# Graph attention on one core: each pair scored and mixed one step behind its decoding, with two gather buffers and two closing pairs

## The chip, the cores and the metric

The kernel runs on one core of a Trainium2 chip. The metric is the time of one execution on the device in microseconds (us), the median of several executions. A difference of about 0.2% (1.6 us) is what a measurement of this kernel can tell from none.

## What is computed

A layer of graph attention over 8192 nodes with 128 features, and a 0/1 matrix of 8192 x 8192 integers that says who is whose neighbour:

```python
h = jnp.maximum(_layernorm(x, axis=-1), 0.0)
s_i = h @ attn[:d]
s_j = h @ attn[d:]
e = leaky_relu(s_i + s_j.T, negative_slope=0.2)
e = e + jnp.where(adj > 0, 0.0, -1e9)
out = x + softmax(e, axis=1) @ h
```

The matrix is 256 MB. Each row has on average four neighbours, so the softmax of a row runs over a handful of nodes once they are known.

## The kernel before

**Start.** The nodes are read (4 MB), normalised in four quarters, and multiplied with the attention vectors. The result, `h` with its scores, is written to a table in DRAM, `h_table`, from which neighbours are later gathered.

**Stream.** The adjacency is read in 64 tiles of 128 rows, each in two halves of 2 MB. The halves are numbered n = 0 to 127 here; tile t has halves 2t and 2t+1, and two tiles make a pair p (halves 4p to 4p+3), so there are 32 pairs. A ring of five half buffers (`adj_ring`) takes the loads, which are issued on SP's queue (`load_pair`). The load of half n+5 is issued when ScalarE (ACT) has turned half n into signs (`sign_tile`, which also counts the row's neighbours).

**Decoding.** TensorE packs the signs of a tile into code words (`pack_tile`; three tiles in PSUM), VectorE (DVE) takes the largest words (`max_tile`), and after the pair's second tile derives from them the numbers of up to twelve neighbours for the pair's two rows in each partition (`find_pair`, whose last result is `near_id`). GpSimd (POOL) then issues twelve indirect DMAs that fetch these rows of `h_table` into a buffer of the ring `near` (`gather_pair`).

**Scoring and mixing.** `score_pair` (DVE) adds scores over the gathered rows and ends with `below`; `exp_pair` (ACT) makes the weights; `weigh_mix` and two `add_row` (DVE) sum the weighted rows and add x, which counts up `pair_mixed`. SP stores the pair. Pair g is scored in DVE's step g+2 (the table `MIXES`), between the two `max_tile` of that step, and mixed in the same step, around `flag_pair`. ACT computes its weights in the step after that, behind the first of four halves. The ring `near` has three buffers; gather p waits until pair p-3 is mixed.

**The rest.** Rows with too many neighbours for twelve slots go to a list of 128 rows for each eight pairs (the deep list: `find_deep`, `gather_m`, `score_deep`, `exp_m`, `add_deep`, `store_m`). Rows without a neighbour form the lone batch, in the last pairs (`lone_mark` to `lone_end`); its partial sums are added by `lone_add`, and TensorE's `rank_pair` of some pairs waits for that, because both use the same PSUM bank. The last three pairs (`CLOSING`) are not mixed by DVE: DVE's `weigh_pair` gives weights, ACT writes 16 diagonal matrices a pair (`write_diagonals`), TensorE multiplies (`mix_pair`), ACT copies out (`close_pair`). After the stream come the last deep list, a loop for rows that fit nowhere (one short round here) and the rest of the lone batch.

**Order.** Every engine's program is written out by hand in its own block, in order; semaphores are the only links. In one step p, DVE runs `lone_begin`, `max_tile(2p)`, scoring, `max_tile(2p+1)`, `key_pair`, `find_pair(p)`, the first row's sum, `flag_pair(p)`, `find_deep`, the lone batch, the second row's sum. The rows of the profile carry line numbers of the code below: L614 is the sign, L631 `exp_pair`, L770 `max_tile`, L822 `near_id`, L907 the first instruction of `score_pair`, L923 `below`, L1017 the first of `score_deep`, L1158 `lone_add`, L1367 `pack_tile`, L1385 `rank_pair`, L521 `gather_pair`.

## Time and profile before

| | us |
|---|---|
| median of three executions | 815.76 (815.68 to 815.86) |
| the profiled execution | 813.88 |
| its span, first to last instruction | 812.1 |
| ScalarE busy | 534.3 |
| VectorE busy | 615.4 |
| TensorE busy | 368.9 |
| GpSimd busy | 504.5 |

The profile is one execution. Its page gives busy times, the span in 40 slices of 20.3 us, the chain of work that ended last, and the costliest groups. The timeline lists instructions in order of time; each row has a start, a duration, the engine, the line, what is written and read, and in brackets how long the engine idled ahead of it and what released it.

### The profile page before, as it was taken

The numbers are of one execution on the slowest core, as the hardware profiler recorded it, in microseconds if no ns is written. First come the engines' busy times: TensorE is split into PE (matmuls) and PEld (weight loads), VectorE is DVE, ScalarE is ACT, GpSimd is POOL, SyncE is SP. The second block draws the span as 40 slices with busy tenths as digits, with TensorE's granted clock in tenths as the row PEclk, the third lists the DMA queues.
The fourth block names the chain that finished last, engine by engine and source line by source line (L and its number), as shares of the span: only waits on it lengthen the run. The fifth ranks groups of instructions, "written<-read, shape, count | busy, mean of one in ns | idle before, by whom it ended". The sixth has DMA issues, their size and how long they took to land.

```text
span 812.1 us, 6394 instructions
## 1 busy us (share of the span) xinstructions
PE 368.9 (45%) x1359; PEld 168.9 (21%) x1378; DVE 615.4 (76%) x2028; ACT 534.3 (66%) x410; POOL 504.5 (62%) x526
## 2 busy tenths in 40 slices
PE   1455334444433344444444344443444545646647
PEld 1222011111111111111111011111111213424636
DVE  6898288677758667797769666797769799898933
ACT  4985676676676767676675767667666677767430
POOL 6720777755556767755547677556547667765573
PEclk9875565555555555555555565555555556877679
DMA  8999999999999999999999999999999999993120
GB/s 344 406 408 429 393 406 408 405 414 411 410 391 412 411 408 406 405 406 407 410 403 406 409 407 408 407 412 413 411 412 408 409 407 411 406 410 132 33 56 8
DMA packets 39719, 301.59 MB, mean 371 GB/s; under 512 B 10682, under 2 KB 17149, under 8 KB 22272
## 3 DMA queue, kind: packets, MB, share of 16 engines
q1 hardware_dynamic: 24032, 277.04, 83.9%
q0 software_dynamic: 15360, 23.88, 8.6%
q10 hardware_dynamic: 288, 0.26, 0.1%
q8 instruction: 11, 0.18, 0.1%
q14 instruction: 28, 0.23, 0.1%
HBM read 303.76 MB, written 8.98 MB: 385 GB/s over the span
## 4 chain that ended last, share of the span: by engine, by line
DMA 74%; issue 14%; POOL 5%; ACT 3%; DVE 3%; PE 1%; POOLq 0%; SPq 0%; DVEq 0%
DMA adj_ring<-in_adj_dram 73%; POOL near L521 3%; ACT sign_ring L614 2%; POOL near_m L532 2%; DMA x_all<-in_x_dram 1%; DVE one_hot L725 1%; ACT h_all L626 1%; PE words L1367 0%; DMA out_dram<-adj_ring 0%; POOL out_dram L562 0%; DVE sums L955 0%; DVE cand L770 0%; POOLq L597 0%; DVE terms L950 0%; POOL adj_ring L553 0%
## 5 line engine op out<-in xcount | busy, mean ns | idle before, releaser
L614 ACT ACTIVATE sign_ring<-adj_ring,half_neg 128x4096 fp8e3<-128x4096 int32 x128 | 474.9, 3710 | 215.3 <-DMA adj_ring<-in_adj_dram 215.3
L521 POOL DMA_INDIRECT near<-h_table,near_id x384 | 391.1, 1019 | 234.2 <-issue 122.8
L1367 PE MATMUL words<-sign_ring,pack_w 128*128 128x512 bf16 x511 | 220.2, 581 | 357.9 <-ACT sign_ring L614 357.6
L770 DVE MAX8 cand<-words 128x8 f32<-128x256 f32 x256 | 90.8, 416 | 113.3 <-PE words L1367 113.3
L1367 PEld LDWEIGHTS words<-sign_ring,pack_w 128*128 128x128 bf16 x512 | 53.9, 125 | 520.7 <-ACT sign_ring L614 453.1
L955 DVE TENSOR_REDUCE sums<-terms 128x128 f32<-128x1024 f32 x58 | 112.2, 1935 | 2.0
L532 POOL DMA_INDIRECT near_m<-h_table,id_m x64 | 65.1, 1017 | 19.5 <-issue 19.5
L950 DVE TENSOR_TENSOR terms<-near,weight 128x512 f32<-128x512 f32 (+1 forms) x87 | 73.4, 871 | 0.0
L1358 PE MATMUL words<-place,place_w 128*128 128x512 bf16 x110 | 55.2, 587 | 7.1 <-DVE key L862 3.7
L1393 PEld LDWEIGHTS listing<-cand,one_hot 128*128 128x128 f32 x128 | 33.0, 316 | 10.6 <-issue 7.3
L1348 PE MATMUL listing<-h_all 128*1 128x128 f32 x128 | 18.6, 316 | 24.8 <-ACT h_all L626 24.8
L1393 PE MATMUL listing<-cand,one_hot 128*128 128x34 f32 x128 | 27.6, 358 | 0.2 <-DVE one_hot L866 0.2
L614 ACT ACTIVATION_READ_ACCUMULATOR sign_ring<-adj_ring,half_neg 128x1 f32 x128 | 23.8, 186 | 0.0
L1443 PE MATMUL rank<-h_all,x_all 128*64 128x129 f32 x128 | 21.0, 343 | 4.6 <-DVE key L862 4.6
L787 DVE TENSOR_TENSOR terms<-cand_i,code_mask 128x512 int32<-128x512 int32 x32 | 22.1, 692 | 1.1
L958 DVE SCALAR_TENSOR_TENSOR x_all<-sums,inv,x_all 128x128 f32<-128x128 f32 x58 | 20.4, 351 | 2.1
L756 DVE TENSOR_TENSOR near<-h_all,terms 128x2048 f32<-128x2048 f32 x8 | 21.4, 2681 | 0.0
L644 ACT ACTIVATE adj_ring<-ident,adj_ring 128x128 f32<-128x128 f32 x48 | 14.3, 387 | 10.7 <-DVE adj_ring L970 10.7
L1443 PEld LDWEIGHTS rank<-h_all,x_all 128*64 128x64 f32 x128 | 20.3, 181 | 4.9 <-DVE key L862 4.9
L626 ACT ACTIVATE h_all<-x_all,terms 128x128 f32<-128x128 f32 x48 | 18.8, 480 | 2.3 <-DVE terms L742 2.3
L498 POOL TENSOR_SCALAR h_all<-x_all,terms 128x128 f32<-128x128 f32 x16 | 13.0, 828 | 11.7 <-DVE terms L742 11.7
L907 DVE TENSOR_SCALAR score<-near,h_all 128x8 f32<-128x8 f32 x32 | 7.0, 220 | 17.1 <-DMA near<-h_table,near_id 17.1
(271 smaller groups left out, 521.7 us busy)
## 6 DMA issues: line engine op xcount, KB each, us to landing
adj_ring<-in_adj_dram SPq DMA_DIRECT2D x128, 2048.0 KB, 24.6
near<-h_table,near_id POOLq DMA_INDIRECT x384, 6.4
h_table<-h_all POOLq DMA_DIRECT2D x4, 1056.0 KB, 14.8
x_all<-in_x_dram SPq DMA_DIRECT2D x4, 1024.0 KB, 9.7
out_dram<-x_all SPq DMA_DIRECT2D x30, 128.0 KB, 24.2
near_m<-h_table,id_m POOLq DMA_INDIRECT x64
out_dram<-x_all ACTq DMA_DIRECT2D x2, 128.0 KB, 3.1
adj_ring<-h_table SPq DMA_DIRECT2D x1, 132.0 KB, 2.6
```

The source lines that it names most:

```text
L521: pool.indirect_dma_start(out=near[:, p % RING, k, :], out_offset=None, in_=table, in_offset=bass.IndirectOffsetOnAxis(ap=near_id[:, p % I ...
L532: pool.indirect_dma_start(out=near_m[:, k, :], out_offset=None, in_=table, in_offset=bass.IndirectOffsetOnAxis(ap=id_m[:, k:k + 1], axis=0 ...
L614: nc.scalar.activation(bytes_of, adj_ring[:, n % HALVES, :].rearrange("p (d r i) -> p d r i", r=2, i=WORDS), ACT.Sign, bias=half_neg[:, :] ...
L626: nc.scalar.activation(h_all[:, t, 0:D], x_all[:, t, :], ACT.Relu, bias=shift[:, t:t + 1], scale=rstd[:, t:t + 1]).then_inc(h_ready, 1)
L770: last = nc.vector.max(out=cand[:, p % 2, t % 2, 8 * q:8 * q + 8], in_=words[t % 3][:, q * PART:(q + 1) * PART])
L787: nc.vector.tensor_tensor(codes[:, :, :, :].rearrange("p a w c -> p (a w) c"), cand_i[:, :, :].rearrange("p a w -> p (a w)").unsqueeze(2). ...
L950: nc.vector.tensor_tensor(terms[:, at, :], near[:, e, slots, 0:D], weight[:, g % 2, weights].unsqueeze(2).broadcast_to([P, at.stop - at.st ...
L955: nc.vector.tensor_reduce(sums[:, a, :], terms[:, :, :].rearrange("p k d -> p d k"), AX.X, ALU.add).then_inc(mixing, 1)
L1358: nc.tensor.matmul(at[:, k * BANK:(k + 1) * BANK], place_w[:, :], place[:, k * BANK:(k + 1) * BANK], start=True, stop=False)
L1367: last = nc.tensor.matmul(at[:, k * BANK:(k + 1) * BANK], pack_w[:, d, :], twins[:, o + k * BANK:o + (k + 1) * BANK], start=False, stop=(d ...
L1393: last = nc.tensor.matmul(listing[:, 0:REC], one_hot[:, p % 2, a, :], cand[:, p % 2, a, :], start=(p % SEG == 0 and a == 0), stop=(p % SEG ...
L1443: last = nc.tensor.matmul(lone_sum[b], part[:, k * e:(k + 1) * e], h_all[:, c * lt + k, 0:ONE + 1], start=(first and k == 0), stop=(final ...
```

## The change

Every pair is scored in step g+1 instead of g+2, and not between the two `max_tile` but behind `find_pair`. The mixing follows behind `flag_pair` and the lone batch's step, both rows together. The deep list is scored behind the pair's scores, and summed at the end of the step instead of ahead of `max_tile(2p+1)`; its weights are computed by ACT directly behind those of a pair, and its store is moved one step back on POOL. ACT computes the weights of pair g in step g+2 instead of g+3, again behind the first half. `near` has two buffers and shares a tensor, `gathered`, with the deep list's buffer `near_m`, because the scratch for the start (`products`) needs more room than two buffers. Only the last two pairs are left to TensorE; pair 29 is mixed by DVE in step 30.

```diff
-    CLOSING = 3
+    CLOSING = 2
-    RING = 3
+    RING = 2
-        near = sb("near", [P, RING, SLOTS, COLS], fp32)
-        near_m = sb("near_m", [P, DEEP, COLS], fp32)
+        gathered = sb("gathered", [P, (RING * SLOTS + DEEP) * COLS], fp32)
+        near = gathered[:, 0:RING * SLOTS * COLS].rearrange("p (e k c) -> p e k c", e=RING, k=SLOTS)
+        near_m = gathered[:, RING * SLOTS * COLS:].rearrange("p (k c) -> p k c", k=DEEP)
-        products = near[:, :, :, :].rearrange("p e k c -> p (e k c)")
+        products = gathered
-        MIXES = {p: [p - 2] for p in range(2, PAIRS)}
...
             for p in range(PAIRS):
-                if p >= SEG and p % SEG == DEEP_MIX:
+                if p >= SEG and p % SEG == DEEP_MIX + 1:
                     store_m(p // SEG - 1)
...
             def exp_step(p):
-                for g in MIXES.get(p, []):
-                    exp_pair(g)
-                for c in early_parts(p - 1 - FIRST_STEP):
-                    exp_lone(0, c)
+                if p >= 1:
+                    exp_pair(p - 1)
+                if p >= SEG and p % SEG == DEEP_MIX:
+                    exp_m(p // SEG - 1)
             for p in range(1, PAIRS):
                 sign_tile(2 * p, (0,))
+                for c in early_parts(p - 2 - FIRST_STEP):
+                    exp_lone(0, c)
                 exp_step(p - 1)
                 sign_tile(2 * p, (1,))
-                sign_tile(2 * p + 1, (0,))
-                if p >= SEG and p % SEG == DEEP_MIX:
-                    exp_m(p // SEG - 1)
-                sign_tile(2 * p + 1, (1,))
+                sign_tile(2 * p + 1)
...
-                    dve.wait_ge(near_zeroed, 1)
+                    dve.wait_ge(near_zeroed, 2)
...
                 lone_begin(p)
                 max_tile(2 * p)
                 if p in (1, PAIRS - 1):
                     key_pair(p - 1)
-                if m >= 0 and p % SEG == DEEP_MIX:
-                    score_deep(m)
-                for g in mixes:
-                    score_pair(g)
-                if m >= 0 and p % SEG == DEEP_MIX:
-                    add_deep(m)
                 max_tile(2 * p + 1)
                 if 1 < p < PAIRS - 1:
                     key_pair(p - 1)
                 find_pair(p)
-                if p < PAIRS - 1:
-                    for g in mixes:
-                        weigh_mix(g)
-                        add_row(g, 0)
+                score_pair(p - 1)
+                if m >= 0 and p % SEG == DEEP_MIX:
+                    score_deep(m)
                 flag_pair(p)
...
                 lone_step(p)
-                for g in mixes:
-                    add_row(g, 1)
+                weigh_mix(p - 1)
+                add_row(p - 1, 0)
+                add_row(p - 1, 1)
+                if m >= 0 and p % SEG == DEEP_MIX:
+                    add_deep(m)
                 lone_close(p)
```

ACT at the start, from half 2 on: x11 stands for eleven halves in a row, ACT_TABLE_LOAD and L631 are the first pair's weights. Before:

```order
L614 ACTIVATE sign_ring,degree<-adj_ring,half_neg 128x2x2x1024 x11
L631 ACT_TABLE_LOAD
L631 ACTIVATE weight<-below 128x16
L614 ACTIVATE sign_ring,degree<-adj_ring,half_neg 128x2x2x1024 x4
L631 ACTIVATE weight<-below 128x16
```

And of the changed kernel:

```order
L614 ACTIVATE sign_ring,degree<-adj_ring,half_neg 128x2x2x1024 x7
L631 ACT_TABLE_LOAD
L631 ACTIVATE weight<-below 128x16
L614 ACTIVATE sign_ring,degree<-adj_ring,half_neg 128x2x2x1024 x4
L631 ACTIVATE weight<-below 128x16
```

The first weights, which wait for pair 0's scores, now stand behind half 8 instead of half 12.

DVE in step 1, from the end of `find_pair(1)` on (L834 to L856 are `flag_pair`, L770 `max_tile(4)`). Before:

```order
L822 TENSOR_TENSOR near_id<-offset,unused 128x12 [waits find]
L824 TENSOR_REDUCE missing<-invalid 128x2
L834 SCALAR_TENSOR_TENSOR lacking<-missing,degree 128x2 [waits signed,flags_ready,find]
...
L856 TENSOR_TENSOR prior<-prior,flag 128x1 [waits flagging]
L770 MAX cand<-words 128x8 [waits listed,packed]
L770 MAX cand<-words 128x8 x3
L907 TENSOR_SCALAR score<-near,h_all 128x8 [waits near_in0]
```

Of the changed kernel (L902 to L918 are the same scores, L829 to L851 the same flags):

```order
L817 TENSOR_TENSOR near_id<-offset,unused 128x12 [waits find]
L819 TENSOR_REDUCE missing<-invalid 128x2
L902 TENSOR_SCALAR score<-gathered,h_all 128x8 [waits near_in0]
...
L918 TENSOR_TENSOR below<-leaky,top 128x16 [waits scoring]
L829 SCALAR_TENSOR_TENSOR lacking<-missing,degree 128x2 [waits signed,flags_ready,find]
...
L851 TENSOR_TENSOR prior<-prior,flag 128x1 [waits flagging]
L926 TENSOR_REDUCE total<-weight 128x2 [waits weight_ready]
```

The wait for the first gather (`near_in0`) is now ahead of the flags of pair 1 and of tile 4's `max_tile`.

DVE where step 30 passes into step 31 (`lone_add` is the sum that `rank_pair(30)` waits for). Before:

```order
L955 TENSOR_REDUCE sums<-terms 128x128 [waits mixing]
L958 SCALAR_TENSOR_TENSOR x_all<-sums,inv,x_all 128x128 [waits mixing]
L1158 TENSOR_TENSOR x_all<-x_all,rank 64x129 [waits lone0,lone_summed0]
L1168 RECIPROCAL x_all<-x_all 64x1 [waits lone0]
L1171 SCALAR_TENSOR_TENSOR x_all<-x_all 64x128 [waits lone0,lone_x_in0]
L770 MAX cand<-words 128x8 [waits listed,packed]
```

Of the changed kernel:

```order
L953 SCALAR_TENSOR_TENSOR x_all<-sums,inv,x_all 128x128 [waits mixing]
L1029 RECIPROCAL inv_m<-total_m 128x1 [waits weight_m_ready]
L1031 TENSOR_SCALAR weight_nm<-weight_m,inv_m 128x16 [waits mixing_m]
L1039 TENSOR_SCALAR mixed_m<-gathered,weight_nm 128x128 [waits stored_m,mixing_m]
...
L1049 TENSOR_TENSOR mixed_m<-mixed_m 128x128 [waits mixing_m]
L1153 TENSOR_TENSOR x_all<-x_all,rank 64x129 [waits lone0,lone_summed0]
L1163 RECIPROCAL x_all<-x_all 64x1 [waits lone0]
L1166 SCALAR_TENSOR_TENSOR x_all<-x_all 64x128 [waits lone0,lone_x_in0]
L765 MAX cand<-words 128x8 [waits listed,packed]
```

The deep list's sum (`add_deep`) of step 30 has come between the pair's sum and `lone_add`; before it stood ahead of that step's `max_tile(61)`.

## Rows read from the trace of the kernel before

**Rows 1.** The page, the span in 40 slices: what the DMA engines moved.

```profile
GB/s 344 406 408 429 393 406 408 405 414 411 410 391 412 411 408 406 405 406 407 410 403 406 409 407 408 407 412 413 411 412 408 409 407 411 406 410 132 33 56 8
```

**Rows 2.** The page, the chain of work that ended last, by engine.

```profile
DMA 74%; issue 14%; POOL 5%; ACT 3%; DVE 3%; PE 1%; POOLq 0%; SPq 0%; DVEq 0%
```

**Rows 3.** Timeline of ACT at the start: halves 8, 12, first weights, half 16.

```profile
69.35 3.71 ACT L614 ACTIVATE sign_ring<-adj_ring,half_neg 128x4096 fp8e3<-128x4096 int32 x1 [3.63 <-DMA adj_ring<-in_adj_dram]
...
94.11 3.71 ACT L614 ACTIVATE sign_ring<-adj_ring,half_neg 128x4096 fp8e3<-128x4096 int32 x1 [1.65 <-DMA adj_ring<-in_adj_dram]
...
104.66 0.22 ACT L631 ACTIVATE weight<-below 128x16 f32<-128x16 f32 x1 [5.45 <-DVE below L923]
...
116.86 3.71 ACT L614 ACTIVATE sign_ring<-adj_ring,half_neg 128x4096 fp8e3<-128x4096 int32 x1 [0.91 <-DMA adj_ring<-in_adj_dram]
```

**Rows 4.** Timeline of DVE: pair 0's scores, first and last instruction.

```profile
103.27 0.23 DVE L907 TENSOR_SCALAR score<-near,h_all 128x8 f32<-128x8 f32 x1 [17.06 <-DMA near<-h_table,near_id]
...
104.45 0.17 DVE L923 TENSOR_TENSOR below<-leaky,top 128x16 f32<-128x16 f32 x1
```

**Rows 5.** Timeline of POOL: gather 0, the first and the last of twelve.

```profile
81.84 1.11 POOL L521 DMA_INDIRECT near<-h_table,near_id  x1 [15.05 <-issue]
...
96.29 1.00 POOL L521 DMA_INDIRECT near<-h_table,near_id  x1 [0.30 <-issue]
```

**Rows 6.** The tile `near`: all gathers, from issue to landing.

```profile
DMA to landing us min/median/max: 2.5/6.4/7.9
```

**Rows 7.** Timeline, the first 30 us: SP's first load, DVE, POOL's last clearing.

```profile
0.82 0.39 SPq L405 DMA_DIRECT2D x_all<-in_x_dram  x1
...
5.55 3.19 DVE L725 BATCH_NORM_STATS2 one_hot<-x_all 128x6 f32<-128x128 f32 x16 [4.50 <-DMA x_all<-in_x_dram]
...
13.80 0.20 POOL L487 MEMSET x_m<- 128x128 f32 x1
...
25.85 2.29 DVE L756 TENSOR_TENSOR near<-h_all,terms 128x2048 f32<-128x2048 f32 x1
```

**Rows 8.** Timeline of DVE and ACT in one step of the stream.

```profile
411.80 1.43 DVE L770 MAX8 cand<-words 128x8 f32<-128x256 f32 x4 [6.42 <-PE words L1367]
...
415.47 0.20 ACT L631 ACTIVATE weight<-below 128x16 f32<-128x16 f32 x1
...
416.90 0.17 DVE L822 TENSOR_TENSOR near_id<-offset,unused 128x12 int32<-128x12 f32 x1
...
417.03 3.71 ACT L614 ACTIVATE sign_ring<-adj_ring,half_neg 128x4096 fp8e3<-128x4096 int32 x1 [1.36 <-DMA adj_ring<-in_adj_dram]
```

**Rows 9.** Timeline of DVE, steps 30 and 31.

```profile
721.95 0.34 DVE L1017 TENSOR_SCALAR score_m<-near_m,si_m 128x16 f32<-128x16 f32 x1
...
730.02 1.43 DVE L770 MAX8 cand<-words 128x8 f32<-128x256 f32 x4 [0.40 <-PE words L1367]
...
743.83 0.27 DVE L1158 TENSOR_TENSOR x_all<-x_all,rank 64x129 f32<-64x129 f32 x1
...
751.01 1.43 DVE L770 MAX8 cand<-words 128x8 f32<-128x256 f32 x4 [3.05 <-PE words L1367]
...
755.67 0.17 DVE L822 TENSOR_TENSOR near_id<-offset,unused 128x12 int32<-128x12 f32 x1
```

**Rows 10.** Timeline of TensorE in step 31.

```profile
738.21 2.10 PE L1367 MATMUL words<-sign_ring,pack_w 128*128 128x512 bf16 x8
...
744.24 0.16 PE L1385 MATMUL rank<-flag,before 128*128 128x2 bf16 x1 [3.57 <-DVE x_all L1158]
...
745.10 1.91 PE L1367 MATMUL words<-sign_ring,pack_w 128*128 128x512 bf16 x4
```

**Rows 11.** The page's group of diagonals, 16 of them a closing pair.

```profile
L644 ACT ACTIVATE adj_ring<-ident,adj_ring 128x128 f32<-128x128 f32 x48 | 14.3, 387 | 10.7 <-DVE adj_ring L970 10.7
```

**Rows 12.** Timeline after the stream: pair 31's gather arrives (TensorE), the last store (POOL).

```profile
773.82 0.49 PE L1403 MATMUL words<-x_all,ident 128*128 128x128 f32 x2 [1.51 <-DMA near<-h_table,near_id]
...
809.37 0.98 POOL L562 DMA_INDIRECT out_dram<-adj_ring  x1 [7.12 <-DVE adj_ring L1171]
```

More of the change, by code:

```diff
@@ L426, in _ @@
                 load_pair(p)
-                for g in MIXES.get(p - 2, []):
-                    store_pair(g)
+                if p >= 4:
+                    store_pair(p - 4)
             for g in range(PAIRS - 4, BODY + 1):
@@ L672, in exp_step @@
             def exp_step(p):
-                for g in MIXES.get(p, []):
-                    exp_pair(g)
-                for c in early_parts(p - 1 - FIRST_STEP):
-                    exp_lone(0, c)
+                if p >= 1:
+                    exp_pair(p - 1)
+                if p >= SEG and p % SEG == DEEP_MIX:
+                    exp_m(p // SEG - 1)
             for p in range(1, PAIRS):
                 sign_tile(2 * p, (0,))
+                for c in early_parts(p - 2 - FIRST_STEP):
+                    exp_lone(0, c)
                 exp_step(p - 1)
                 sign_tile(2 * p, (1,))
-                sign_tile(2 * p + 1, (0,))
-                if p >= SEG and p % SEG == DEEP_MIX:
-                    exp_m(p // SEG - 1)
-                sign_tile(2 * p + 1, (1,))
+                sign_tile(2 * p + 1)
+            act.wait_ge(signed, 4 * PAIRS)
             exp_step(PAIRS - 1)
-            act.wait_ge(signed, 4 * PAIRS)
             write_diagonals(BODY)
+            close_pair(BODY)
+            for c in range(LONE_PARTS[LAST]):
+                exp_lone(LAST, c)
             exp_pair(BODY + 1)
-            close_pair(BODY)
             write_diagonals(BODY + 1)
@@ L693, in _ @@
             store_pair(BODY + 1)
-            for c in range(LONE_PARTS[LAST]):
-                exp_lone(LAST, c)
-            exp_pair(BODY + 2)
-            write_diagonals(BODY + 2)
-            close_pair(BODY + 2)
-            store_pair(BODY + 2)
             act.wait_ge(sizes_ready, 2)
@@ L1231, in _ @@
             for p in range(1, PAIRS):
-                mixes = MIXES.get(p, [])
                 m = p // SEG - 1
@@ L1270, in _ @@
                 lone_step(p)
-                for g in mixes:
-                    add_row(g, 1)
+                weigh_mix(p - 1)
[3 more added lines that the diff above has]
+                    add_deep(m)
                 lone_close(p)
-            score_pair(BODY + 2)
-            weigh_pair(BODY + 2)
+            score_pair(BODY + 1)
+            weigh_pair(BODY + 1)
             dve.wait_ge(sizes_ready, 2)
@@ L1494, in _ @@
             mix_pair(BODY + 1)
-            mix_pair(BODY + 2)
             pe.wait_ge(pair_mixed, PAIRS)
```

2 lines of the change are left out of this document (removed).

## The prediction

> **What bounds the kernel now.** I read the page's slices first. From the second slice to the 36th the DMA engines move about 408 GB/s without a break [rows 1], and the chain that ended last is DMA for 74% of the span, nearly all of it the adjacency [rows 2]. So up to some 746 us the kernel is its stream: the engines matter there only where they hold a buffer so long that the stream runs dry, and time lost by a dry stream is not given back, since it already runs at its full rate. Then I read the two places where the chain is not the stream. At the start ACT wastes 5.45 us in front of the first weights [rows 3], because DVE waits 17.06 us for gather 0 [rows 4], which POOL could not start before 81.84, when the table had been written [rows 5]. At the end the last half is signed and the time runs from `near_id` of pair 31 at 755.84 [rows 9] over its gather, which lands at about 773.8 and is waited for by TensorE [rows 12], to the last store at 809.37 [rows 12]: one serial chain of 56 us. Whatever delays this `near_id` delays the end by as much.
>
> **The start: a stall of the stream.** Pair 0's weights move from behind half 12 to behind half 8. ACT ends half 8 at 69.35 + 3.71 = 73.1 [rows 3] and then waits until pair 0 is scored; behind this wait stand the signs of all further halves, and behind these the loads: load n+5 is issued when half n is signed. Before, ACT met the wait at about 98 and lost 5.45 us there, with the loads up to 17 already issued, and nothing ran dry: half 16 came at 116.86 [rows 3]. Now halves 9 to 13 fill the ring. Halves land every (116.86 - 94.11) / 4 = 5.69 us [rows 3], so half 13 lands at 94.11 + 5.69 = 99.8, and then there is no load left in any queue.
>
> When does ACT go on? The last of gather 0's twelve DMAs is issued at 96.29 [rows 5], and the score began at 103.27 [rows 4], 7.0 us later; all gathers took 2.5 to 7.9 us to land, 6.4 in the median [rows 6]. The table is not ready earlier than before. So the gather lands between 98.8 (2.5 us) and 103.3 (as before); I take 101, since the stream that it competes with ends at 99.8. The score takes 104.62 - 103.27 = 1.35 us [rows 4], the weights 0.2: half 9 is signed from 102.5 to 106.2, and load 14 is issued at 106.3. What a load takes that finds the queue empty is not in the stream; the nearest row is the first of all: 1 MB of x, issued at 0.82 and used at 5.55, 4.73 us [rows 7]. At 410 GB/s the bytes are 2.5 of it, so 2.2 are start-up; 2 MB then take 5.1 + 2.2 = 7.3 us, and half 14 lands at 113.6. Before it landed at 94.11 + 2 x 5.69 = 105.5: **8.1 us late**. Some comes back: during the gap, 99.8 to 108.5, POOL goes on with gather 1, one DMA in 1.3 us (14.45 us for eleven intervals [rows 5]) of 128 x 132 x 4 bytes, together 0.45 MB, which later need no time of the stream: 1.1 us. Net **+7.0 us**, between 4.8 (landing at 98.8) and 10.4 (at 103.3, nothing given back).
>
> A single load from an empty queue is also priced by the Trainium skill, "DMA: Bandwidth & Descriptors", section "Anatomy of one DMA — SWDGE (gpsimd) path": about 2.0 us plus the bytes over 436 GB/s, given for DMAs issued by GpSimd. By that estimate half 14 takes 6.8 us and the sum is 0.5 lower; the row of 4.73 us for 1 MB against its 4.4 bears it out nearly.
>
> **The stream after that.** In each step ACT now waits for scores that come late: in the step shown the words are ready at 411.80, `near_id` ends at 417.07 and the score would end at 418.5, while ACT stands at the place of the weights at 415.47 and signed the next half at 417.03 [rows 8]. So ACT loses 3.1 us and the half is 1.8 late. This costs nothing while the ring covers it: a half takes 3.71 against 5.69 of the stream, two halves later ACT is on time, and loads are issued five halves ahead. Without that cover ACT's loop would bind: three halves 11.1, packing 2.1, 411.80 to 417.07 5.3, score 1.4, weights 0.2, together 20.1 us a step against the stream's 4 x 5.69 = 22.8. It fits, with 2.7 us to spare; the deep list's work, at most twice the block of 7.67 us [rows 9] in eight steps, is under the 21 us that these have to spare. The same margin brings ACT back after the stall: half 13 is signed by 102.5 + 20.1 + 3.8 = 126.4, load 18 goes out then, and load 17 lands at 113.6 + 3 x 5.69 = 130.7, so there is no second gap. The gathers: twelve issues take 15.4 us, the landing 6.4 [rows 5, 6], 21.8 us within a step of 22.8. The score behind `find_pair` thus just finds its rows, and the second buffer is enough in the stream. I take **0** here; bounds below.
>
> **The end: DVE's work comes late.** In step 30 the deep scores, a pair's scores and the deep sum stood ahead of `max_tile(61)`, from 721.95 to 729.62 (730.02 less 0.40 idle), 7.67 us, and ended 0.40 us before the words came [rows 9]: they cost nothing. Now all three stand behind `find_pair(30)`, whose time the words set as before. From there to `lone_add` at 743.83 DVE had no idle time, so `lone_add` now starts at 743.83 + 7.67 = 751.5. TensorE's `rank_pair(30)` waits for it: at 744.24 before (3.57 us idle for it) [rows 10], at 751.9 now. Queued behind it on TensorE is tile 63: its filling starts 0.86 after, then come eight packing matmuls. They take 2.10 us (a row of eight) or 2 x 1.91 [rows 10]; I take 3.8, because at this very place, after idling, four took 1.91, and the idle time is longer now. So the words are ready at 756.6 instead of 751.01 [rows 9]: **+5.6 us**, or +3.9 with the fast row. `find_pair(31)` follows, 4.83 us as before.
>
> **Behind that.** The score of pair 30 (1.35) now stands ahead of the flags, so the weights for its diagonals come up to 1.35 us later, and through TensorE also the lone batch's numbers, for which DVE waits; before, DVE was ready at the very time at which gather 31 landed. 0 to 1.35, taken as **0.4**. That one closing pair less is written (16 diagonals, 14.3 / 3 = 4.8 us of ACT [rows 11]) saves nothing: ACT and TensorE wait for gather 31 in any case [rows 12]. Pair 29's mixing on DVE takes the place of pair 28's in step 30 and is in the 743.83. Its and the others' stores: SP gets one more, at the end, before it waits for sizes; POOL's deep store moves ahead of gathers 15, 23 and 31, about 1.3 us when POOL waits for `near_id`. The longer wait at the start (`near_zeroed`) ends at 14.0, the products begin at 25.85 [rows 7]; uncovered it would cost nothing up to 11.8 us. These are nothing.
>
> **Sum.** 7.0 + 5.6 + 0.4 = 13.0 us. The profiled execution took 813.88 and would take 826.9; it stands 1.9 under the median, so from the median 815.76 the forecast is **828.8 us**. The parts' lower ends give 815.76 + 8.7 = 824.5, the upper ones 815.76 + 17.4 = 833.1.
>
> **Rivals.**
> Only the start costs: the block of step 30 finds cover that I don't see (words later, or DVE ahead), 815.8 + 7.0 = 822.8. For it: DVE idles 3.05 us ahead of the last `max_tile` [rows 9]. Against: 7.67 is more than that.
> Only the end costs: the stream makes up the gap, 821.8. For it: nothing but the five halves of cover. Against: the slices show no spare rate [rows 1].
> Two buffers are enough and no wait ends late: 815.8. For it, the 21.8 us of a gather in a step of 22.8; against it, the first gather, held by the table. The Trainium skill, "Trainium Kernel Development and Optimization", section "Best Practices", says to double-buffer so that transfers and work overlap; by that rule this is the outcome, and the trace agrees for the stream's steps, not for the first.
> ACT's loop becomes the bound: if gathers land as late as the slowest (7.9 us [rows 6]), 15.4 + 7.9 = 23.3 is over the step's 22.8, scores wait, and with 1 us more in each of 28 steps the time is 815.8 + 13 + 28 = 857. It decides where a step's loop passes 22.8.
> Faster: the start is covered, and the end is set by the diagonals' work on ACT rather than by gather 31; 4.8 us less, 811. It decides only if gather 31 lands before pair 30 is closed, which it does not: TensorE waited 1.51 us for it after closing two pairs [rows 12].
>
> **Chances.** Both costs as forecast 0.72, start alone 0.09, end alone 0.06, no change 0.05, loop bound 0.05, faster 0.03. The range 821 to 836 holds the first and the next two nearly whole (0.83); the loop's case, the unchanged and the faster are left out. A measurement can tell about 0.2% (1.6 us) from no change: slower by more 0.92, within it 0.05, faster 0.03.
>
> **What would show it.** In the profile after: a wait of about 30 us of ACT for `below` from 73 on; the GB/s of the fifth or sixth slice clearly under 390, and no other such slice before the end; half 16 about 8 us later than 116.86; in later steps waits of ACT of 2 to 6 us without loss of rate. At the end `rank_pair(30)` waiting for `lone_add`, and 10 to 11 us from the last sign's start (745.89 before, shifted) to the last `max_tile`, where it was 5. It is wrong if the slices stay flat at the start, if a second gap or a lower rate follows, or if `near_id` of pair 31 comes less than 12 us after the last sign's start.

## The result and the profile after

The changed kernel takes 831.79 us in the median (830.33 to 832.3, 4 runs), the kernel before, run beside it, 815.81: a ratio of 1.0195 [1.018, 1.0209], slower by 16.0 us. A second set of runs gave 1.0201 [1.0184, 1.0219]. The forecast was 828.8 us in a range of 821 to 836.

The page of after: its GB/s in 40 slices of 20.8 us, and the chain that ended last by engine.

```profile
GB/s 335 403 409 416 306 334 408 407 413 408 412 410 408 409 407 406 412 409 411 413 405 411 406 406 408 410 411 416 411 410 413 404 411 382 397 357 44 30 48 9
...
DVE 27%; POOL 21%; DMA 18%; issue 16%; ACT 10%; PE 8%; ACTq 0%; DVEq 0%; POOLq 0%
```

Before, the stream ran level [rows 1] and DMA was 74% of the chain [rows 2]. Now slices 5 and 6 have a hole, slices 34 to 36 sag (382, 397, 357), and the chain runs through DVE, POOL's gathers and ACT. The waits of after say the same (engine, line, waited for: us in total, times, longest):

```profile
ACT weight L631 <- DVE below L918: 203.0, 32, 27.2
...
ACT sign_ring L614 <- DMA adj_ring<-in_adj_dram: 48.5, 28, 3.6
DVE score L902 <- DMA gathered<-h_table,near_id: 47.3, 18, 17.2
```

ACT waits for the score of each of the 32 pairs, and for the stream in only 28 of 128 halves. The wait of 27.2 is the start; on ACT's timeline of after it stands behind half 8, while in [rows 3] the first weights waited 5.45 us behind half 12:

```profile
70.20 3.71 ACT L614 ACTIVATE sign_ring<-adj_ring,half_neg 128x4096 fp8e3<-128x4096 int32 x1 [3.60 <-DMA adj_ring<-in_adj_dram]
...
102.47 0.21 ACT L631 ACTIVATE weight<-below 128x16 f32<-128x16 f32 x1 [27.17 <-DVE below L918]
102.59 3.69 ACT L614 ACTIVATE sign_ring<-adj_ring,half_neg 128x4096 fp8e3<-128x4096 int32 x1
```

By the windows of after (busy us of PE, PEld, DVE, ACT, POOL; then granted clock, DMA share, GB/s) the DMA engines go dry at that point; in the windows of 10 us behind it, up to 740, the rate is at no place under 363:

```profile
90.00:100.00 10.00, 0.00 (x0) 0.00 (x0) 0.00 (x0) 0.00 (x0) 7.87 (x8) 0.50 0.91 355
100.00:110.00 10.00, 2.74 (x6) 0.74 (x6) 8.48 (x22) 7.53 (x6) 7.87 (x8) 0.50 0.30 97
110.00:120.00 10.00, 6.57 (x16) 1.65 (x16) 6.34 (x23) 7.46 (x5) 3.10 (x4) 0.50 1.01 414
```

Against the 406 GB/s around it, that is 10 x (51 + 309) / 406 = 8.9 us without stream.

The end of after, timelines of ACT, DVE and TensorE, which answer to [rows 9, 10]: the last half's signing, `lone_add`, the last two `max_tile`s, `near_id` of pair 31, and `rank_pair(30)` with tile 63 behind it.

```profile
757.33 3.70 ACT L614 ACTIVATE sign_ring<-adj_ring,half_neg 128x4096 fp8e3<-128x4096 int32 x1
...
763.41 0.28 DVE L1153 TENSOR_TENSOR x_all<-x_all,rank 64x129 f32<-64x129 f32 x1
...
764.26 1.41 DVE L765 MAX8 cand<-words 128x8 f32<-128x256 f32 x4
768.36 1.43 DVE L765 MAX8 cand<-words 128x8 f32<-128x256 f32 x4 [2.12 <-PE words L1355]
...
773.02 0.17 DVE L817 TENSOR_TENSOR near_id<-offset,unused 128x12 int32<-128x12 f32 x1
...
763.84 0.16 PE L1373 MATMUL rank<-flag,before 128*128 128x2 bf16 x1 [8.65 <-DVE x_all L1153]
...
764.70 3.62 PE L1355 MATMUL words<-sign_ring,pack_w 128*128 128x512 bf16 x8
```

For the rest of this text the profiled execution is cut at four points of the traces: the starts of the signings of halves 8, 112 and 127 (the last) on ACT, and of `near_id(31)` on DVE; the last column reaches to the end of the span. Ratios are to the kernel before, timed in the same set; they are of medians, while the stretches are of one execution each, which can stand 2 us and more from its median (e7 at 819.60 against 821.88, e1 at 833.36 against 830.86).

| kernel | to 8 | 8 to 112 | 112 to 127 | 127 to near_id | behind | ratio [interval] |
|---|---|---|---|---|---|---|
| before | 69.4 | 592.1 | 84.5 | 9.8 | 56.4 | 1 |
| after | 70.2 | 599.1 | 88.0 | 15.7 | 57.6 | 1.0195 [1.018, 1.0209] |
| after again (e12) | 68.7 | 598.7 | 87.7 | 15.7 | 57.6 | 1.0201 [1.0184, 1.0219] |
| e1, three buffers | 70.3 | 600.6 | 88.4 | 15.3 | 57.0 | 1.0182 [1.0158, 1.0205] |
| e4, before, pair 0 early | 70.7 | 602.5 | 84.5 | 10.5 | 56.9 | 1.0118 [1.0091, 1.0144] |
| e7, start two behind | 68.8 | 589.9 | 87.6 | 14.9 | 56.5 | 1.0115 [1.0097, 1.0133] |
| e2, exp one half later | 70.1 | 597.3 | 84.4 | 15.4 | 56.5 | 1.0143 [1.0125, 1.0162] |
| e11, lone batch halved | 68.8 | 598.3 | 84.3 | 15.4 | - | - |
| e10, deep gathers 6, 5, 5 | 68.8 | 603.5 | 87.0 | 15.7 | 58.1 | 1.0297 [1.028, 1.0314] |
| e3, deep sum early | 70.3 | 600.4 | 90.5 | 9.8 | 56.5 | 1.0135 [1.0111, 1.0159] |
| e6, lone_add first | 68.8 | 597.8 | 86.4 | 13.2 | 56.7 | 1.0162 [1.0145, 1.0179] |
| e5, e2 and e3 | 68.8 | 597.3 | 85.3 | 14.5 | 57.5 | 1.0117 [1.0097, 1.0136] |
| e8, e2, e3 and e7 | 68.8 | 592.0 | 83.9 | 14.0 | 57.4 | 1.0043 [1.0026, 1.006] |
| e9, e8 and 6, 5, 5 | 68.8 | 590.9 | 83.8 | 12.1 | 57.3 | 1.0046 [1.0029, 1.0063] |

The medians of the kernel before in the four sets were 815.81, 816.31 (e1 to e4), 812.67 (e5 to e8) and 812.95 (e9 to e12), so times of different sets are compared by their ratios, and a us in the column "8 to 112" between sets says little. An expected time stands on the scale of a kernel before at about 816; a ratio times 815.8 puts a measured one on it. After less before is 7.0 + 3.6 + 5.9 + 1.1 and 0.9 ahead of half 8, together 18.5 us of span; of e12 it is 6.6 + 3.2 + 5.9 + 1.1 less 0.6, together 16.3, near the 16.0 of the medians.

The stretch from half 112 to 127 is cut by signings, and these are not the stream there. The load of half 127 in after, from SP's timeline, with its time to landing, and ACT's weights in the last step:

```profile
736.22 0.33 SPq L414 DMA_DIRECT2D adj_ring<-in_adj_dram  x1
...
DMA to landing us min/median/max: 18.7/18.7/18.7
...
748.50 0.22 ACT L631 ACTIVATE weight<-below 128x16 f32<-128x16 f32 x1 [4.92 <-DVE below L918]
749.73 0.22 ACT L635 ACTIVATE weight_m<-below_m 128x16 f32<-128x16 f32 x1 [1.01 <-DVE below_m L1023]
```

The half lies ready at 754.9 and is signed from 757.33, because ACT waited for the two weights with three signings still ahead of it. So ACT is 2.4 us behind the stream at the last half in after, 3.4 in e12, 7.7 in e10 and 5.8 in e3; in the kernel before, e2, e4, e8, e9 and e11 it signs the half as it lands. Counted by landings, the loads lose only 1.2 us from half 112 to 127 in after, 1.6 in e1 and nothing in e12.

### The profile page after: what moved, and what is told of

The parts are those of the page before. It is cut to its first block, busy times and chain, and to the rows that moved or that the text cites. A ratio compares the mean times of both kernels' runs of the same rounds, so it can differ in the third digit from the quotient of the medians.

```text
span 830.6 us, 6311 instructions
## 1 busy us (share of the span) xinstructions
PE 366.4 (44%) x1323; PEld 169.6 (20%) x1342; DVE 621.2 (75%) x2034; ACT 523.0 (63%) x393; POOL 525.1 (63%) x526
## 4 chain that ended last, share of the span: by engine, by line
DVE 27%; POOL 21%; DMA 18%; issue 16%; ACT 10%; PE 8%; ACTq 0%; DVEq 0%; POOLq 0%
POOL gathered L521 18%; ACT sign_ring L614 9%; DMA adj_ring<-in_adj_dram 9%; DMA gathered<-h_table,near_id 7%; DVE cand L765 3%; PE words L1355 3%; DVE sums L950 3%; POOL gathered L532 2%; DVE gathered L751 2%; PE words L1431 2%; DMA h_table<-sums 2%; DVE terms L945 2%; PE words L1395 1%; DVE terms L782 1%; DVE one_hot L720 1%
## 5 line engine op out<-in xcount | busy, mean ns | idle before, releaser
L521 POOL DMA_INDIRECT gathered<-h_table,near_id x384 | 412.7, 1075 | 235.4 <-issue 125.1
L1355 PE MATMUL words<-sign_ring,pack_w 128*128 128x512 bf16 x511 | 216.7, 573 | 364.5 <-ACT sign_ring L614 364.2
L631 ACT ACTIVATE weight<-below 128x16 f32<-128x16 f32 x32 | 6.9, 215 | 203.0 <-DVE below L918 203.0
L950 DVE TENSOR_REDUCE sums<-terms 128x128 f32<-128x1024 f32 x60 | 115.9, 1932 | 2.1
L532 POOL DMA_INDIRECT gathered<-h_table,id_m x64 | 66.1, 1033 | 19.5 <-issue 19.5
L945 DVE TENSOR_TENSOR terms<-gathered,weight 128x512 f32<-128x512 f32 (+1 forms) x90 | 74.7, 857 | 0.0
L902 DVE TENSOR_SCALAR score<-gathered,h_all 128x8 f32<-128x8 f32 x32 | 7.8, 244 | 47.4 <-DMA gathered<-h_table,near_id 47.3
L1431 PE MATMUL rank<-h_all,x_all 128*64 128x129 f32 x128 | 23.1, 366 | 5.8 <-DVE key L857 5.8
L614 ACT ACTIVATION_READ_ACCUMULATOR sign_ring<-adj_ring,half_neg 128x1 f32 x128 | 23.9, 187 | 0.0
L1431 PEld LDWEIGHTS rank<-h_all,x_all 128*64 128x64 f32 x128 | 22.3, 195 | 6.0 <-DVE key L857 6.0
L782 DVE TENSOR_TENSOR terms<-cand_i,code_mask 128x512 int32<-128x512 int32 x32 | 22.2, 693 | 1.1
L751 DVE TENSOR_TENSOR gathered<-h_all,terms 128x2048 f32<-128x2048 f32 x8 | 21.4, 2676 | 0.0
```

The source lines that it names most:

```text
L521: pool.indirect_dma_start(out=near[:, p % RING, k, :], out_offset=None, in_=table, in_offset=bass.IndirectOffsetOnAxis(ap=near_id[:, p % I ...
L532: pool.indirect_dma_start(out=near_m[:, k, :], out_offset=None, in_=table, in_offset=bass.IndirectOffsetOnAxis(ap=id_m[:, k:k + 1], axis=0 ...
L614: nc.scalar.activation(bytes_of, adj_ring[:, n % HALVES, :].rearrange("p (d r i) -> p d r i", r=2, i=WORDS), ACT.Sign, bias=half_neg[:, :] ...
L751: nc.vector.tensor_tensor(prods, h_all[:, c * XT:(c + 1) * XT, 0:D], attn_b[:, a * D:(a + 1) * D].unsqueeze(1).broadcast_to([P, XT, D]), A ...
L782: nc.vector.tensor_tensor(codes[:, :, :, :].rearrange("p a w c -> p (a w) c"), cand_i[:, :, :].rearrange("p a w -> p (a w)").unsqueeze(2). ...
L945: nc.vector.tensor_tensor(terms[:, at, :], near[:, e, slots, 0:D], weight[:, g % 2, weights].unsqueeze(2).broadcast_to([P, at.stop - at.st ...
```

## Experiments: the buffers and the start

**e1: three buffers in the new order.**

```diff
-    RING = 2
+    RING = 3
```

> The changed kernel with three gather buffers instead of two, nothing else (order, closing pairs and mixing as changed). Theory 'order': the gather into a buffer waits for the mixing of the pair two before, and in the new order that mixing ends within the step before, ahead of near_id, so the third buffer frees nothing: 831.8 within 1 us, and DVE's 18 waits for landed gathers (47 us) stay. Rival 'buffers': these waits come from two buffers; then they go, the 3.4 us that the stream lost in the steps with the lone batch come back, and the time is 828 or less.

Measured: 830.86 us, 1.0182; DVE still waits for landed gathers 18 times (41.7 us). The interval covers the changed kernel's ratio: the second buffer is not what costs. What is left is the order and the two closing pairs; the latter were not tested alone, but e8 and e9 below keep them and stand at 1.0043 and 1.0046, so that with all else that is left they cost under 4 us there. This also takes the ground from the rival that rested on double-buffering (the Trainium skill, "Trainium Kernel Development and Optimization", section "Best Practices"): two buffers are indeed enough, and the kernel is slower all the same.

**e4: the kernel before, with pair 0 alone one step earlier.**

```diff
 # ACT, exp_step
-                    exp_pair(g)
+                    if g > 0:
+                        exp_pair(g)
+                if p == 1:
+                    exp_pair(0)
 # DVE, end of the step
                 lone_close(p)
+                if p == 1:
+                    score_pair(0)
```

(Step 2 then leaves out `score_pair(0)`.)

> The kernel before with one move: pair 0 alone is scored at the end of step 1 (DVE) and its exp stands behind half 8 (ACT), as in the changed kernel; all other pairs two steps behind, three buffers. Theory 'start': half 9 is signed from 102.5 us on, load 14 lands 7 to 9 us late, and the stream never gets it back: 823 to 825. Rival 'the ring covers it': 815.8 to 817.

Measured: 826.17 us, 1.0118, and the same hole. ACT's timeline and the windows of e4:

```profile
103.22 0.21 ACT L631 ACTIVATE weight<-below 128x16 f32<-128x16 f32 x1 [27.47 <-DVE below L926]
...
90.00:100.00 10.00, 0.00 (x0) 0.00 (x0) 0.00 (x0) 0.00 (x0) 7.57 (x9) 0.50 0.91 361
100.00:110.00 10.00, 2.74 (x6) 0.74 (x6) 2.08 (x10) 6.78 (x4) 7.87 (x8) 0.51 0.32 77
```

One exp, moved by four halves, makes most of the loss by itself, and the later stretches stay those of before. Its 9.9 us are more than I expected from the start: counted from half 8, half 18 is 8.3 us later than before, and another 2 us come after that, 1.3 of them between halves 30 and 44. There ACT waits for loads alone (its weights wait 28.1 us in all, 27.5 of these at the start), so these 2 us aren't explained.

**e7: the changed kernel, with pairs 0 to 3 two steps behind.**

```diff
 # DVE
+                if 2 <= p <= 5:
+                    score_pair(p - 2)
                 max_tile(2 * p + 1)
...
-                score_pair(p - 1)
+                if p >= 5:
+                    score_pair(p - 1)
...
-                weigh_mix(p - 1)
-                add_row(p - 1, 0)
-                add_row(p - 1, 1)
+                for g in [p - 2] * (2 <= p <= 5) + [p - 1] * (p >= 5):
+                    weigh_mix(g)
+                    add_row(g, 0)
+                    add_row(g, 1)
```

(ACT's `exp_step` in the same way; three buffers.)

> The changed kernel with the start undone: pairs 0 to 3 two steps behind as in the kernel before (scored between the max_tiles of steps 2 to 5), pair 4 and all later ones one step behind; three gather buffers, which alone changed nothing (830.9). Theory 'start': the 8 to 9.5 us of the stream come back, slices 5 and 6 move over 390 GB/s, the rest of the loss (late steps 3.4, end 5.8) stays: 822 to 823.5. Rival 'the loop, not the start': an ACT that waits in every step cannot follow the stream once one-behind begins, and the loss comes later: over 827.

Measured: 821.88 us, 1.0115. Slices 5 and 6 are 399 and 407 GB/s, the stretch from half 8 to 112 is back, and the late stretch, the end and the part behind stay nearly as in the changed kernel. The start is thus shown from both sides: added alone it costs 9.9 us (e4), taken out alone it gives back 1.0195 or 1.0201 less 1.0115, 6.5 to 7 us, where 8 to 9.5 were expected.

## Experiments: the steps with the lone batch

The forecast had nothing for these steps, and the last signing comes 3.2 to 3.6 us later by them in the two profiles of the changed kernel. The size is not steady: in e6 below, whose code is the same up to the end of step 30, it is 1.9.

**e2: the exp one half later.**

```diff
-                exp_step(p - 1)
                 sign_tile(2 * p, (1,))
+                exp_step(p - 1)
                 sign_tile(2 * p + 1)
```

> The changed kernel with ACT's exp of each pair (and of the deep list) one half later in its step: behind both halves of the even tile instead of between them. DVE, PE, POOL and SP keep their order. Theory 'ACT waits in row': at the start half 9 is signed at 74 instead of 102.6, so the first load that comes late is 15 and not 14, some 3.5 us late instead of 8: 4 to 5 us come back; in the steps of the lone batch the wait of the exp (6.6 us a step) shrinks by the 3.7 us of one signing, and the 3.4 us come back: 823 to 825. Rival 'gathers or DVE are the bound of the late steps': only the start gains, 827. Rival 'the start is not the exp's doing': 831.8.

Measured: 827.03 us, 1.0143. The late stretch is whole again (84.4), and the stretch from half 8 is 2 us better, where 4 to 5 were expected. The time is that of the rival by which only the start gains (827), but the gain lies in the late stretch, where that rival has none. The waits of e2:

```profile
ACT sign_ring L614 <- DMA adj_ring<-in_adj_dram: 188.1, 103, 3.7
...
ACT weight L631 <- DVE below L918: 56.1, 11, 21.6
```

ACT waits for the stream again (103 times; 28 in after), so what held the signings back late was the exp waiting in row ahead of them. But the exps of pairs 25 to 28 are hardly closer together than in after: they start at 654.0, 678.4, 700.7 and 724.9, there at 656.8, 681.6, 704.3 and 728.6. What feeds them is slow; with 3.7 us more slack it no longer reaches the last signings.

**e11: the lone batch halved.**

```diff
-    LONE_CAP = (64, 16)
+    LONE_CAP = (32, 16)
```

> The changed kernel with the early lone batch cut from 64 rows to 32 (if more rows are lone, the rest goes to the loop at the very end, and only the stream is read). DVE's three operations of a lone part (1.24 us each) and ACT's exp (1.04) become about half as long: some 1.9 us a step on DVE and 0.5 on ACT, in four parts. Theory 'lone work makes the late loss': the falling back of 3.4 us between half 112 and half 127 shrinks to 1.5 or less. Rival 'gathers make it': it stays at 3.

Measured: more than 32 rows are lone, the loop at the end makes 1600 passes and the time is 23.8 ms; the stream before it can be read. From half 112 to 127 it takes 84.3, as in the kernel before: nothing is lost. (The edit halves ACT's exps of the lone batch too, 1.04 us each, so it doesn't part DVE's share from ACT's.) The step from the exp of pair 25 to that of pair 26, timelines of ACT and DVE, first in e12 (the changed kernel, two lone parts in this step):

```profile
655.25 0.22 ACT L631 ACTIVATE weight<-below 128x16 f32<-128x16 f32 x1 [6.73 <-DVE below L918]
...
679.95 0.21 ACT L631 ACTIVATE weight<-below 128x16 f32<-128x16 f32 x1 [6.77 <-DVE below L918]
...
657.19 0.16 DVE L926 TENSOR_REDUCE total<-weight 128x2 f32<-128x16 f32 x1
...
664.52 1.22 DVE L1134 TENSOR_TENSOR x_all<-x_all,h_all 128x1024 f32<-128x1024 f32 x1
...
670.82 1.26 DVE L1142 SCALAR_TENSOR_TENSOR x_all<-x_all 128x1024 f32<-128x1024 f32 x1
672.00 2.74 DVE L765 MAX8 cand<-words 128x8 f32<-128x256 f32 x8
...
678.43 0.17 DVE L817 TENSOR_TENSOR near_id<-offset,unused 128x12 int32<-128x12 f32 x1
678.60 0.22 DVE L902 TENSOR_SCALAR score<-gathered,h_all 128x8 f32<-128x8 f32 x1
```

and in e11:

```profile
653.16 0.22 ACT L631 ACTIVATE weight<-below 128x16 f32<-128x16 f32 x1 [5.08 <-DVE below L918]
...
675.64 0.21 ACT L631 ACTIVATE weight<-below 128x16 f32<-128x16 f32 x1 [3.78 <-DVE below L918]
...
662.30 0.68 DVE L1134 TENSOR_TENSOR x_all<-x_all,h_all 128x512 f32<-128x512 f32 x1
...
665.87 0.69 DVE L1142 SCALAR_TENSOR_TENSOR x_all<-x_all 128x512 f32<-128x512 f32 x1
666.49 2.74 DVE L765 MAX8 cand<-words 128x8 f32<-128x256 f32 x8
```

In e12 no DVE row of this step bears a wait: weights, mixing, two lone parts (664.52 to 672.0, 7.5 us), both `max_tile`s in one piece (eight MAX8, no wait for words), `find_pair`, score, and the next exp, 24.7 us for a circle that the stream gives 22.8. With the lone parts at 4.2 us it takes 22.5. So one step behind makes DVE's whole step a part of the circle that feeds ACT; two steps behind, ACT found its weights waiting [rows 8].

**e10: the deep list's gathers in three steps instead of four.**

```diff
-    DEEP_PARTS = (4, 4, 4, 4)
+    DEEP_PARTS = (6, 5, 5)
```

> The changed kernel with only the deep list's gathers spread as 6, 5, 5 instead of 4, 4, 4, 4. Theory 'gather queue makes the late loss': the signings no longer fall back by 3.4 us between half 112 and half 127 but by 1 us or less, and with the end's own part 2 to 4 us come back. Rival 'the lone batch's own work on DVE and ACT makes it': the falling back stays 3 us or more, time within 1 us of the changed kernel in the same call.

Measured: 836.46 us, 1.0297, 6.6 us slower than the changed kernel in the same set. Both expectations missed. Gather 28 is free as meant (score(28) waits 3.50 us in e12, not at all here), and the late stretch gains only 0.7 us, though other steps of e10 are later too: the queue of POOL isn't most of what costs there. But elsewhere, where the four parts had just fitted, it now is. Timelines of POOL, DVE and ACT of e10 around pair 11: the last of five deep DMAs and `x_m`, the first of gather 11, its score, its exp.

```profile
317.06 1.00 POOL L532 DMA_INDIRECT gathered<-h_table,id_m  x1 [0.30 <-issue]
318.36 1.00 POOL L537 DMA_INDIRECT x_m<-in_x_dram,row_m  x1 [0.30 <-issue]
319.66 0.99 POOL L521 DMA_INDIRECT gathered<-h_table,near_id  x1 [0.30 <-issue]
...
341.75 0.23 DVE L902 TENSOR_SCALAR score<-gathered,h_all 128x8 f32<-128x8 f32 x1 [4.54 <-DMA gathered<-h_table,near_id]
...
318.39 0.21 ACT L631 ACTIVATE weight<-below 128x16 f32<-128x16 f32 x1 [7.33 <-DVE below L918]
...
343.15 0.22 ACT L631 ACTIVATE weight<-below 128x16 f32<-128x16 f32 x1 [9.78 <-DVE below L918]
```

`near_id(11)` was ready at 314.69; the gather starts 5 us behind it, the score waits 4.54, and the exps are 24.8 us apart. The second such group, at pair 19, is like it (a wait of 4.97, exps 25.1 apart). Slices 26 and 31 dip to 384 and 361 GB/s, but the loads land at half 127 no later than in e12: ACT waits for a load once in the whole execution (3.6 us), and it is the circle through DVE that is late.

**e12: the changed kernel again.**

> The changed kernel itself, beside the three others on the same chip: 1.018 to 1.021 of before, signings 8 to 9 us behind those of before up to half 112 and some 3 us more at half 127. A theory that needs the late 3 us to be an accident of one profile would have them gone here.

Measured: 829.89 us, 1.0201. The late loss is there again (87.7), so it is no accident of one profile.

## Experiments: the end

**e3: the deep list's work back between the two `max_tile`s.**

```diff
                     key_pair(p - 1)
+                if m >= 0 and p % SEG == DEEP_MIX:
+                    score_deep(m)
+                    add_deep(m)
                 max_tile(2 * p + 1)
...
                 score_pair(p - 1)
-                if m >= 0 and p % SEG == DEEP_MIX:
-                    score_deep(m)
```

(Its exp stands between the halves of the odd tile on ACT; the later `add_deep` goes.)

> The changed kernel with the deep list's scores and sum put back between the two max_tiles of their step (and its exp on ACT between the halves of the odd tile), as in the kernel before. Theory 'end' as predicted (5.6 to 5.9 us because the deep sum stands ahead of lone_add and rank_pair(30)): 826. Rival 'the loop takes it back': the deep block now stands ahead of find_pair(30) and so of the score of pair 29, for which ACT waits in the last step; the last half is signed some 5 us later than at 757.3 and the time stays within 1.5 us of 831.8.

Measured: 827.1 us, 1.0135, between the two. The profile is of the slowest of its four runs (829.34). In it, from the last signing to `near_id(31)` it takes 9.8 us, as before the change, but the last signing itself comes 2.5 us later than in after (90.5 against 88.0 from half 112). The 5.9 us of the end come back and 2.5 of them are paid one place earlier, because `find_pair(30)`, and with it the score for which ACT waits, now stands behind the deep block. By the ratios 4.9 us are gained in all.

**e6: `lone_add` ahead of the deep sum.**

```diff
-                lone_begin(p)
+                if p < PAIRS - 1:
+                    lone_begin(p)
...
                 add_row(p - 1, 1)
+                if p == PAIRS - 2:
+                    lone_begin(p + 1)
                 if m >= 0 and p % SEG == DEEP_MIX:
                     add_deep(m)
```

> The changed kernel with one move on DVE: in the last step the lone batch's add and end (3 small operations) stand ahead of the deep sum of step 30 instead of behind it. DVE's work in the row stays the same. Theory 'rank_pair waits': rank_pair(30) comes at 759 instead of 763.8, tile 63 is packed by 763, and only DVE's row stays late: near_id(31) 2.5 to 3 us earlier, 828.5 to 829. Rival 'DVE's row is all of it': near_id(31) as before, 831.3.

Measured: 825.76 us, 1.0162; `near_id(31)` 13.2 us behind the last signing (753.04) instead of 15.7. Timelines of DVE and TensorE of e6:

```profile
753.68 0.28 DVE L1153 TENSOR_TENSOR x_all<-x_all,rank 64x129 f32<-64x129 f32 x1
...
759.61 1.42 DVE L765 MAX8 cand<-words 128x8 f32<-128x256 f32 x4
761.59 1.40 DVE L765 MAX8 cand<-words 128x8 f32<-128x256 f32 x4
...
754.10 0.16 PE L1376 MATMUL rank<-flag,before 128*128 128x2 bf16 x1 [2.02 <-DVE x_all L1153]
...
754.96 3.81 PE L1358 MATMUL words<-sign_ring,pack_w 128*128 128x512 bf16 x8
```

The words of tile 63 are ready at 758.8 and the last `max_tile` no longer waits for them; it waits its turn behind the deep sum. So of the 5.9 us, 2.5 were `rank_pair(30)` and tile 63 held behind the deep sum, as forecast; the rest is DVE's row.

**e5, e8, e9: the edits together.** e5 is e2 and e3, e8 is e5 with e7's start and three buffers, e9 is e8 with e10's number. In part:

```diff
 # e5, ACT
+                sign_tile(2 * p, (1,))
                 exp_step(p - 1)
-                sign_tile(2 * p, (1,))
...
 # e5, DVE, ahead of max_tile(2 * p + 1)
+                    score_deep(m)
+                    add_deep(m)
...
 # e8
+                if 2 <= p <= 5:
+                    score_pair(p - 2)
...
 # e9
-    DEEP_PARTS = (4, 4, 4, 4)
+    DEEP_PARTS = (6, 5, 5)
```

> The changed kernel with two earlier edits together: the exp one half later in each step, and the deep list's scores and sum between the two max_tiles. Alone they gave 827.0 and 827.1 us. Theory 'additive': the later exp takes away the wait through which the early deep block delayed the last signings (last half at 761.2 instead of 757.3), so the end's 5.9 us come back whole beside the 4.8 us: 821 to 822, the last half signed at 752 to 753, near_id(31) 10 us behind it. Rival 'the loop takes it': the deep block still delays the score of pair 29 and with it the last signings by 4 us: 824 to 826.

> The changed kernel with all three edits: start two steps behind (pairs 0 to 3), exp one half later, deep work between the max_tiles; three buffers, two closing pairs. Theory 'three places': nothing of the loss is left but what stands behind near_id(31) (1.2 us in the trace): 815.5 to 818. Rival 'one step behind costs in every step': over 820.

> The kernel with all three edits (start two behind, exp one half later, deep work between the max_tiles; it gave 1.0043 of before) with one number more changed: the deep list's 16 gathers are spread over three steps as 6, 5, 5 instead of over four as 4, 4, 4, 4, so that none of them stands ahead of the gather of pair 28. Theory 'gather queue': gather 28 starts at once behind near_id(28) (4.3 us earlier), score(28) waits no more (3.57 us), DVE's row of the last two steps is that much earlier, near_id(31) comes 10 to 11 us behind the last signing's start instead of 14.0: 1.000 to 1.002 of before. Rival 'DVE's row of one step behind (score, exp's round trip, mixing in one piece) is what is late': 14 us stay, 1.004.

Measured: 1.0117, 1.0043 and 1.0046. e5 gave 10.1 us over before where additivity wanted 6 to 7, and so the time of the rival (825.3 on the scale of the expectation); the last two stretches together, from half 112 to `near_id(31)`, show why: 94.2 in the kernel before, 103.7 in after, 99.9 with e2, 100.2 with e3, and 99.7 with both. By the ratios the gains are 4.2 us for e2, 4.9 for e3 and 6.4 for both: each edit alone takes most of what the two take. I read late loss and end as one late DVE and not as two places; ACT's wait in the last step, shown above, fits that. e8 confirms that the start adds to that (1.0117 to 1.0043), and 4 us of end remain, so that "three places" is not the whole of it: 819.3 on the scale of the expectation, over its 818. The rest of the row, timelines of DVE and ACT of e9 (pair 28's score and weights, the deep list's exp):

```profile
711.36 0.23 DVE L905 TENSOR_SCALAR score<-gathered,h_all 128x8 f32<-128x8 f32 x1 [0.28 <-DMA gathered<-h_table,near_id]
...
715.48 0.17 DVE L929 TENSOR_REDUCE total<-weight 128x2 f32<-128x16 f32 x1 [1.64 <-ACT weight L631]
...
725.62 0.21 ACT L635 ACTIVATE weight_m<-below_m 128x16 f32<-128x16 f32 x1 [5.17 <-DVE below_m L1026]
```

In e8 that score waited 3.57 us for gather 28, here 0.28, and the end shrinks from 14.0 to 12.1 in the profiles: this much was POOL's queue. The time did not follow (1.0046 against 1.0043); e9's profile is of its fastest run (814.68 against a median of 816.39), so a gain is not shown, and the number is the rival's. The mixing still begins 4.6 us after `near_id(29)` (710.84), by way of score and exp; in the kernel before it began 0.2 us behind it (711.91 and 711.75). ACT then waits 5.17 us for the deep scores of the next step, with the signings behind it. What the last 2.3 us of the end and 0.9 behind it consist of was not separated further. No version of these beats the kernel before.

## Why the prediction was right, and where it was short

The sign, the place of the main costs and the range held; the sum was 3 us short (13.0 against 16.0).

**Start, forecast 7.0.** The steps of it came as worked out: half 9 from 102.5 (measured 102.59), half 13 signed by 126.4 (122.49 + 3.70 = 126.2), no second gap. The engines stood dry for 8.9 us (forecast: half 14 late by 8.1), and from half 8 to 112 the kernel lost 7.0 and 6.6 us in the two profiles of it. One term was too small: half 14's load, the first into the empty queue, landed 8.5 us after its issue (8.3 in e12), not 7.3. SP's timeline of after and its time to landing:

```profile
106.41 0.33 SPq L414 DMA_DIRECT2D adj_ring<-in_adj_dram  x1
...
DMA to landing us min/median/max: 8.5/8.5/8.5
```

By half 112 the loads were back to 7.0 and 7.1 us late, so more was given back than the 1.1 reckoned, and the agreement of the 7.0 is in part luck. That some of the gap is given back fits these numbers; that it is the gathers' bytes was not tested. The estimate by the Trainium skill ("DMA: Bandwidth & Descriptors", section "Anatomy of one DMA — SWDGE (gpsimd) path"), 6.8 us for this load, is 1.7 short of the 8.5 measured, and the measured time holds here, with gather 1 beside the load and half 15's issued 3.7 us behind it. One of the signs named beforehand was wrong: half 16 came 16.7 us later (133.56), not 8. ACT itself was behind there, with loads in the ring, so that its lag at one half was no measure of the stream's loss; the load of half 16 landed 8.5 us later than before (125.3 against 116.8).

**Stream afterwards, forecast 0.** This is the step that failed. The circle of 20.1 us a step was right where no gather is waited for (exps at 102.47 and 122.36, 19.9 apart; 22.2 where one is). But the sum asked only whether the deep list's work fits in the margin of 2.7 us, and left out the lone batch in steps 26 to 28, whose parts take 3.7 us each of DVE, two of them in step 26. With them the working's own sum is 23.8 for one part and 27.5 for two, more than the stream's 22.8. Measured, in e12, were 24.7 with two, and 22.6 and 23.9 with one, both with a wait for the gather in them (2.32 and 3.50); without that wait, in e10, a step with one part took 20.1, since the part falls into DVE's idle time. Two steps ahead of the first stands one of 26.4 (exps of pairs 23 and 24), with `find_deep` and the marking of the lone rows in it. e11 shows that the lone batch is needed for the loss, e2 that it acts through ACT's exp. The stream proper came out near its 0: what failed is "two halves later ACT is on time", for after these steps ACT was still 2.4 and 3.4 us behind the loads at the last half, and nothing came behind it to make that up. The sign "no other such slice before the end" failed with it (slices 34 and 36 at 382 and 357). It measures 3.2 to 3.6 us in the two profiles, 1.9 in e6.

**Gathers "within a step".** From the end of `near_id` to the last landing it took 22.7 us in the mean of pairs 2 to 29 in after, not 21.8, and steps aren't even (21.4 to 26.8): 18 scores waited for their rows, up to 4 us behind the start. e10 shows how thin it is: one or two DMAs more ahead of a gather cost 6.6 us in all. There ACT hardly ever waits for a load, so that the rival by which ACT's loop becomes the bound is one or two DMAs away from this kernel.

**End, forecast 5.6; 5.9.** The rows of after carry each step: `lone_add` behind the deep sum, `rank_pair(30)` 8.65 us idle for it, tile 63 packed in 3.62 (3.8 taken), 11.0 us from the last signing to the last `max_tile` (10 to 11 named). But the prediction read it as a stall that the deep block's place makes. e6 confirms this for 2.5 us only: with the stall gone, the deep sum still stands in DVE's row ahead of the last `max_tile`, a second path 2.5 us shorter that the sum didn't name. That 5.6 and 5.9 agree so well holds for the path taken, not for what removing it would give. e3 shows that moving the block back moves part of the lateness to the signings, and in e5, e8 and e9 the end keeps 12.1 to 14.5 us instead of 9.8.

**Behind, forecast 0.4.** 1.1 in both profiles, within the bounds 0 to 1.35; with other edits it was between 0.1 and 1.6, so nothing finer can be read.

## What to carry over

When a consumer is moved one step closer to its producer, write down the closed circle that this makes (here exp, mixing, lone part, `max_tile`s, `find_pair`, score, exp, on two engines that each work in order) and add to it everything that stands in these queues in any step, not only in the ordinary ones; what counts is a run of long steps, above all one that ends with the stream, since nothing behind it makes the lateness up. In a kernel that its stream bounds, look at the first pass separately: a wait that costs nothing in the steady state holds up the loads when the first data can't be there yet. And when either of two edits brings back a good part of two late places, these may be one late engine: test the edits together before adding them up.

## What the runs showed of the hardware

On POOL an indirect gather DMA is issued every 1.30 us (1.0 busy, 0.30 between), but twelve of them beside the full stream took 15.3 to 17.8 us in after, not evenly 15.3, because single ones took 1.3 to 2.3. I hadn't reckoned with this spread, and a step has under 1 us to spare for it. A 2 MB load into an empty queue took 8.5 us to land in after; in the running stream of the kernel before a load came every 5.69. The same kernel before had medians of 816.31 and 812.67 us in two sets of runs on different chips, 0.4% apart and more than several of the effects here, so that only ratios within a set could be used.
